# Half of the next expert's W1l made by GpSimd instead of VectorE in a mixture-of-experts kernel

## What is computed

```python
x = x + tanh(g_xattn) * xattn(layernorm(x), ctx)
t = rmsnorm(layernorm(x)) * norm_w
logits = t @ gate_w.T + gate_b
vals, idx = top_k(logits, 4); G = softmax(vals) scattered to (tokens, 16)
h = einsum('mh,eoh->emo', t, w1) + b1            # 512 -> 2 x 512 per expert
act = a * sigmoid(1.702 * a) * (b + 1)           # a = min(h[::2], 7), b = clip(h[1::2], -7, 7)
y = einsum('emi,edi->emd', act, w2) + b2
x = x + tanh(g_ffn) * einsum('me,emd->md', G, y)
```

## Time and profile before

| | |
|---|---|
| median of 3 runs | 849.4 us (849.01 to 851.18) |
| the profiled execution | 844.8 us, span of the core 843.0 us |
| mean granted clock of TensorE | 0.965 of full |
| busy: TensorE, VectorE, ScalarE, GpSimd | 91%, 60%, 53%, 37% of the span |
| VectorE's W1l in the loop (line 1028) | 60 x 1219 ns |
| ScalarE's W1h in the loop (line 703) | 60 x 1054 ns |
| GpSimd's W1l in the first stage (line 1097) | 3 x 2356 ns |
| DMA | 117.00 MB, mean 139 GB/s |

### The profile page before, as it was taken

The page is one execution under the profiler, slowest core; times in us unless marked ns, Lnnn a source line. Parts: engine busy times, 40 slices in busy tenths (PEclk is TensorE's granted clock), DMA queues, the critical chain, the costliest instruction groups (busy, mean ns, idle before and its releaser), DMA issues.

```text
span 843.0 us, 16501 instructions
## 1 busy us (share of the span) xinstructions
PE 770.3 (91%) x3972; PEld 641.6 (76%) x3973; DVE 503.6 (60%) x1006; ACT 446.5 (53%) x771; POOL 311.6 (37%) x290
## 2 busy tenths in 40 slices
PE   5999998058999999999999999999999999999984
PEld 2555555047888899988888888898998988898873
DVE  2677675416676575566576665756556575746540
ACT  3455534025566564556557655646556565656540
POOL 0257665631324315242324323324333334325212
PEclk9999998559999999999999999999999999999997
DMA  8566653052577576347649655556535555544312
GB/s 290 180 199 217 208 167 113 5 137 75 130 210 168 108 221 162 62 130 206 138 148 229 174 108 126 148 135 154 145 60 150 108 151 139 150 124 75 37 25 38
DMA packets 107767, 117.00 MB, mean 139 GB/s; under 512 B 11808, under 2 KB 77344, under 8 KB 107744
## 3 DMA queue, kind: packets, MB, share of 16 engines
q1 hardware_dynamic: 88896, 77.32, 29.7%
q0 software_dynamic: 18848, 39.40, 23.8%
HBM read 88.06 MB, written 28.94 MB: 139 GB/s over the span
## 4 chain that ended last, share of the span: by engine, by line
PE 80%; DVE 7%; issue 4%; ACT 3%; POOL 2%; DMA 1%; DVEq 0%; ACTq 0%; POOLq 0%
PE ps L525 37%; PE ps L474 25%; PE ps L378 7%; PE ps L389 7%; PE ps L453 3%; POOL tab L1093 2%; DVE W1l L1028 1%; DVE uu L1017 1%; DVE hv L1019 1%; PE ps L406 1%; DVE bv L1015 1%; ACT hTh L698 1%; ACT bw L678 1%; PE ps L397 1%; DVE ps L988 1%
## 5 line engine op out<-in xcount | busy, mean ns | idle before, releaser
L525 PE MATMUL ps<-xTh,W1h 128*128 x768 | 257.8, 336 | 14.3 <-issue 7.9
L525 PE MATMUL ps<-xTl,W1h 128*128 x768 | 251.9, 328 | 0.0
L525 PE MATMUL ps<-xTh,W1l 128*128 x768 | 251.7, 328 | 0.0
L1175 POOL DMA_INDIRECT out<-ys,dgI x75 | 118.8, 1584 | 307.2 <-ACT ys L657 283.7
L525 PEld LDWEIGHTS ps<-xTh,W1h 128*128 128x128 f32 x768 | 145.7, 190 | 25.3 <-issue 20.3
L525 PEld LDWEIGHTS ps<-xTh,W1l 128*128 128x128 f32 x768 | 145.7, 190 | 5.5
L525 PEld LDWEIGHTS ps<-xTl,W1h 128*128 128x128 f32 x768 | 145.9, 190 | 5.0
L474 PE MATMUL ps<-W2h,hTh 128*128 x300 | 119.8, 399 | 7.7 <-DVE hTl L1023 7.7
L474 PE MATMUL ps<-W2l,hTh 128*128 x300 | 117.5, 392 | 0.0
L474 PE MATMUL ps<-W2h,hTl 128*128 x300 | 117.4, 391 | 0.0
L657 ACT ACTIVATE ys<-ps,dgI 128x512 f32<-128x512 f32 x75 | 51.7, 690 | 123.5 <-DVE ps L988 123.5
(11 more groups left out here) (130 smaller groups left out, 999.8 us busy)
## 6 DMA issues: line engine op xcount, KB each, us to landing
W1f<-in_wts SPq DMA_DIRECT2D x64, 512.0 KB, 4.7
W2f<-in_wts SPq DMA_DIRECT2D x32, 512.0 KB, 6.9
X<-in_x SPq DMA_DIRECT2D x8, 512.0 KB, 6.5
Kt<-in_ctx SPq DMA_DIRECT2D x8, 512.0 KB, 4.4
Vt<-in_ctxT SPq DMA_DIRECT2D x8, 512.0 KB, 4.0
rows<-tt SPq DMA_DIRECT2D x8, 512.0 KB, 3.0
out<-base SPq DMA_DIRECT2D x8, 512.0 KB, 3.0
b2s<-in_bias SPq DMA_DIRECT2D x16, 256.0 KB, 9.1
```

Source lines behind the costliest of these rows:

```text
L525: m = e.matmul(P_[i % 2][:, 0:32 * w], (W1h, W1l)[wl][:, i, 2 * k + h, :], (xTh, xTl)[xl][:, bass.ds(par, 1), k, 0:32 * w], start=(t == 0) ...
L1175: e.indirect_dma_start(out, bass.IndirectOffsetOnAxis(dgI[:, j, 0:1].bitcast(I32), axis=0), ys[j][:], None, compute_op=ALU.add).then_inc(d ...
```

## The change

In every last unit, the low parts of chunks 2 and 3 of the next expert's W1 (the third and the fourth) are made by GpSimd and no longer by VectorE. GpSimd does it at the end of its iteration, behind the gathers, and waits for the same high parts as VectorE did. It counts them on `e_lop`, which stands at 3 after the first stage. TensorE waits for `e_lo1` before parts 0 and 1 and for `e_lop` before parts 2 and 3, and SyncE does likewise before its reloads. GpSimd now loads all six fields of a unit into registers, where it had three.

```diff
@@ sp
-                    e.wait_ge(e_lo1, N1 * (x_ - 1) + c + 1)
+                    e.wait_ge(*((e_lo1, N1 + 2 * (x_ - 2) + c + 1) if c < 2 else (e_lop, 3 + 2 * (x_ - 2) + c - 1)))
                     load_w(x_, c)
@@ pe
-                    made, read = e.snap(x_ * N1 + (i + 1)), e.snap(u * 4 + (i + 1))
+                    read = e.snap(u * 4 + (i + 1))
                     if i == 0:
                         e.wait_ge(e_xl, ready)
-                    e.wait_ge(e_lo1, made)
+                    e.wait_ge(e_lo1 if i < 2 else e_lop, e.snap(x_ * 2 + (3 + i if i < 2 else i)))
@@ dve, pairs
                         low_h(i, w)
-                        low_w(i)
+                        if i < 2:
+                            low_w(i)
@@ pool, loop
                 place(row(fut), e.snap(u + 3))
                 gathers(fut)
+                with e.If(e.snap(now[F_LAST], min_val=0, max_val=1) > 0):
+                    x_ = e.snap(now[F_X], min_val=0, max_val=E - 1)
+                    for c in range(2, N1):
+                        e.wait_ge(e_hi1, e.snap(x_ * N1 + (N1 + c + 1)))
+                        e.tensor_tensor(W1l[:, c, :, :], W1f[:, c, :, :], W1h[:, c, :, :].bitcast(F32), ALU.subtract).then_inc(e_lop, 1)
                 for regs, came in ((was, now), (now, nxt), (nxt, fut)):
                     for a, q in zip(regs, came):
                         e.reg_mov(a, q)
-                load_fields(e, fut, e.snap(u + 3), F_NT)
+                load_fields(e, fut, e.snap(u + 3), 0)
```

More of the change, by code:

```diff
@@ L1130, in pool @@
             n = units(e)
-            was, now, nxt, fut = many_regs(e, "pool_was", 3), many_regs(e, "pool_now", 3), many_regs(e, "pool_nxt", 3), many_regs(e, "pool_fut", 3)
+            was, now, nxt, fut = many_regs(e, "pool_was", 6), many_regs(e, "pool_now", 6), many_regs(e, "pool_nxt", 6), many_regs(e, "pool_fut", 6)
             given, added = e.alloc_register("pool_given"), e.alloc_register("pool_added")
@@ L1134, in pool @@
             e.reg_mov(added, 0)
[L1135 to L1139, removed]
+            for r in was:
+                e.reg_mov(r, 0)
+            load_fields(e, now, 0, 0)
+            load_fields(e, nxt, 1, 0)
+            load_fields(e, fut, 2, 0)
             def row(regs):
-                return e.snap(regs[2], min_val=0, max_val=(E + 1) * TE - 1)
+                return e.snap(regs[F_ROW], min_val=0, max_val=(E + 1) * TE - 1)
             def count(regs):
-                return e.snap(regs[0], min_val=0, max_val=4)
+                return e.snap(regs[F_NT], min_val=0, max_val=4)
             def gathers(regs):
```

## The result

The changed kernel takes 909.5 us (908.2 to 912.1), the one before 849.2 us: the ratio is 1.071 (1.068 to 1.074), so the change costs 60 us where 39 were forecast. The direction was as forecast, and so was the main cause, GpSimd's subtractions holding up VectorE's chain to the last hTl. The time lies above the range, because TensorE's clock, which the sum left out, cost 18.6 us more than before.

The account below looks back on a forecast made before the run. TensorE, 91% busy, was taken as the bound, VectorE counting only where TensorE waits for the last hTl. Waits of 39.0 us less 1 us relief gave +38 on the 849.4 median: 888 us, range 861 to 903.

Parts of the forecast that it names:

- Relief, 1 us: VectorE without two W1l subtractions per last unit: bv gains about 0.16 us in six narrow units, 1.0 us in all.
- rival 3: Faster: the chain to hTl pays for chunk 2 in full, six narrow units x 1.22 = 7.3 us, 842; chance 0.07.
- The waits, 39.0 us: GpSimd's subtractions hold VectorE's chain to the last hTl, delaying TensorE's second layer; 39.0 us over 15 last units.
- The clock, left out of the sum: TensorE's clock falling behind new waits, about 1.7 us per stretch, up to nine: up to 15 us, in the range only.
- Queueing at nothing: On GpSimd, the copy into dgI queued behind the two subtractions delays no scaling by ScalarE: costed at nothing.
- rival 4: GpSimd late: dgI held behind both products, ScalarE's first scaling waits, 2 us in each of 15 units, 918; chance 0.03.
- Rivals 1 and 2: 1: VectorE-GpSimd lock weaker or products better placed, 868 us, chance 0.16; 2: they don't disturb each other, 848 us, chance 0.08.

Follow-up runs that it names:

- experiment 1: Changed kernel with GpSimd's two subtractions cut to 8 of their 1024 columns, all waits and counts kept: 850.4 us, ratio 1.001.
- experiment 5: Changed kernel with the second of GpSimd's two subtractions held back until the fourth hTl is made: 867.2 us, ratio 1.017.
- experiment 3: Kernel before plus two GpSimd fills of 128x2048 behind the gathers of each last unit, VectorE still making all four chunks: 854.3 us, ratio 1.002.
- experiment 7: Changed kernel with both subtractions behind the fourth hTl; chunk 2 there, chunk 3 behind W2l; both behind W2l: 861.2, 857.7, 868.2 us.

## Why the prediction was right and wrong

*Relief, 1 us*: right. It is just under 1 us (experiment 1), far from the 7.3 us of rival 3.

*The waits, 39.0 us*: 41.8 us measured, close as a sum and partly by luck: four units came out some 9 us above their forecasts in all, the others some 6 us below. Unit by unit, the wait before the second layer grew by:

| unit | 0 | 1 | 2 | 3 | 5 | 6 | 7 | 8 | 9 | 11 | 13 | 15 | 17 | 19 | 21 |
|---|---|---|---|---|---|---|---|---|---|---|---|---|---|---|---|
| forecast | 0.9 | 0.8 | 3.7 | 4.0 | 0 | 2.7 | 3.5 | 0.9 | 4.1 | 2.5 | 2.5 | 3.6 | 3.65 | 2.5 | 3.65 |
| measured | 4.1 | 4.1 | 2.8 | 3.2 | 1.3 | 1.8 | 3.0 | 2.3 | 3.5 | 2.3 | 2.3 | 1.5 | 3.7 | 2.3 | 3.7 |

Units 11, 13, 17, 19 and 21 (384 wide) are right to 0.2 us, but that is luck too. I had let the hTl of i=2 through and held bv between the products; in fact that hTl stood through both products (5.41 us in unit 17), and bv and the rest followed. Either way two products and one bv of 0.36 us lie before uu, so the sum comes out alike.

Units 0, 1, 5 and 8 failed, on two steps. I placed the products at the old end of the gathers. The third of unit 1's four gathers was stretched beside VectorE's third W1l, to 1.45 us; with that gone it takes 0.95 us, and the four together 4.83 us instead of 5.49, so the products moved forward from hv onto bv. In units 5 and 8 such a gather went from 1.91 and 1.92 us to 0.99 and 0.98: the products of unit 5 now begin 0.32 us before the last hTl, which I had as over by then, and hold it for 4.82 us. Removing an operation moved what it had been holding up. And I took it that an operation that has begun or asked first gets its turn; in units 0, 1 and 8 bv, begun 0.57, 0.62 and 0.15 us before the products, stood through both of them (5.67 us in unit 1). That they were held for both and not for one is experiment 5's finding.

The wide units 2, 3, 6, 7 and 9 came out 0.5 to 0.9 us too high. Unit 15 came out 2.1 us too high: I took it for a wide one, and it is 384 wide. There each product met an hTl and held it for only about 2 us.

*The clock, left out of the sum*: this is the step that failed and the reason the time is out of range. I had the price, 1.7 us for each stretch at half clock from the earlier trace rows, and allowed nine stretches in the upper bound only, on the ground that a wait of 1.28 us had not brought one. The loss was 18.6 us, as much as eleven stretches of 1.7 us: the price was right, and the number of them was put at nothing in the sum. The waits that I forecast, 2.5 to 5 us, lie mostly between the two rows that I had, 1.28 us without a stretch and 4.50 us with one, so there was no ground for taking the first. With 1.7 us in each of the eleven units that I had costed at 2.5 us or more, the sum would have been 849.4 + 38 + 18.7 = 906. That it comes so close is luck in part: units 3, 15 and 19 were among the eleven and had no stretch, units 0 and 1 were not and had one, and unit 9 had twice the length.

*Queueing at nothing*: right where the change put it: TensorE's new waits are all for hTl, and the fills of experiment 3 cost 2 us. A late GpSimd costs all the same where the work stands ahead of the scatters and gathers (experiment 7), by late gathers and not by the late dgI of rival 4.

*Rivals 1 and 2*: no; in every one of the 15 units a VectorE operation stood still until a product had ended.

## What to carry to other kernels

Before work is moved to an idle engine, ask what it shares with the engine it relieves, and look for a row where the two already run side by side: here one 8-element operation of 2.17 us told it. Cost the idle time that a change gives TensorE twice, once as the wait and once as the clock behind it (here 41.8 us and 18.6 us). And where an engine's busy time is no bound, as VectorE's 60% here, relieving it is worth only what the next wait in line leaves: less than 1 of 36.6 us.

## What the hardware did that I had not expected

- By the recorded starts, a VectorE operation that has already begun is stopped by a GpSimd subtraction: hTl begun 0.28 us before took 5.41 us, bv begun 0.62 us before took 5.67 us. With one subtraction in place of two in a row it is 3.11 us (experiment 5).
- That happened only where the subtraction came directly (0.03 us) behind a gather. Where GpSimd had stood still before it, an operation that had begun kept its time, and in unit 15 it was the subtraction that took longer, 2.81 us instead of 2.4 (timeline of the changed kernel):

```profile
683.23 0.56 DVE L1019 SCALAR_TENSOR_TENSOR hv<-sg,uu 128x384 f32<-128x384 f32 x1
683.24 2.81 POOL L1189 TENSOR_TENSOR W1l<-W1f,W1h 128x1024 fp32r<-128x1024 f32 x1 [0.34 <-issue]
...
684.37 2.09 DVE L1023 TENSOR_TENSOR hTl<-hv,hTh 128x384 fp32r<-128x384 f32 x1 [0.58 <-ACT hTh L698]
```

  And the bv of unit 1, which takes 0.43 us when it is free, would have been over 0.19 us before the recorded start of the subtraction that held it. So the recorded starts do not tell which of the two had asked first, and what decides it stays open.
- Fills on GpSimd leave two-input operations alone (0.69 us beside a fill of 1.82 us), but hold the one-input bv (1.83 us for 0.43). This is what the Trainium skill says of it (SBUF — State Buffer, section "Who interferes with whom"): two SBUF inputs contend with GpSimd's reads and not with instructions that only write, two-port modes with both. The trace agrees on the first count; it agrees on the second if bv runs in such a mode, which it does not show. It also says that whoever issues first keeps the pair for the whole instruction; hv in unit 15 (first by 0.01 us, not held) fits that by its recorded start and hTl in unit 17 (first by 0.28 us, held) does not, and since the records do not show which was issued first, no run here decides it.
- VectorE in turn stretches GpSimd's gathers: 1.45 us beside a W1l of VectorE, 0.95 us without, and 1.91 us against 0.99 in unit 5.
